# Gated cross-attention and quantised feed-forward on one core: the first two tiles laid out anew

## What is computed

```
q = Wq @ xn + bq            # [64, 512]
k = Wk @ cn + bk
v = Ws @ s + bs
attn = softmax(q^T k)       # [512, 512], over its last axis
mean = v @ attn^T ;  sq = (v*v) @ attn^T
x1 = x + tanh(g0) * (cn * sqrt(relu(sq - mean^2)) + mean)
x2 = x1 + tanh(g1) * layernorm(x1) @ w^T     # w = (weight_q - 8) * scale + zero, [512, 512]
```

## Time and profile before

| what | us |
|---|---|
| median of 3 runs (lowest to highest) | 186.06 (185.04 to 186.35) |
| the profiled execution's own time | 186.42 |
| its span, first to last instruction | 184.6 |
| busy: PE, DVE, ACT, POOL | 167.2, 141.0, 118.0, 120.4 |

### The profile page before, as it was taken

One profiled execution on the slowest core, in us unless ns is written; L12 is line 12 of the kernel. 1 busy time (PEld: TensorE's weight loads), 2 busy tenths in 40 slices (PEclk: granted clock), 3 DMA queues, 4 the chain that ended last, 5 costly groups with the idle time before them and its releaser, 6 DMA issues.

```text
span 184.6 us, 3489 instructions
## 1 busy us (share of the span) xinstructions
PE 167.2 (91%) x1128; PEld 147.1 (80%) x1128; DVE 141.0 (76%) x311; ACT 118.0 (64%) x261; POOL 120.4 (65%) x145
## 2 busy tenths in 40 slices
PE   1554999999999999999999999999999979789992
PEld 0432889999999999999999999998789867567881
DVE  2897696689859887986988798676159679988851
ACT  2253575978598678859867885995569995232110
POOL 1455586917955896799589679944328959966310
PEclk9999999999999999999999999999999999999999
DMA  6408566883796699679679966356100000111212
GB/s 169 166 21 202 186 159 138 237 201 86 184 319 153 155 287 245 162 216 286 139 170 249 283 145 153 78 134 151 44 0 0 4 0 0 57 62 60 111 57 114
DMA packets 14321, 25.75 MB, mean 139 GB/s; under 512 B 2336, under 2 KB 2464, under 8 KB 14304
## 3 DMA queue, kind: packets, MB, share of 16 engines
q1 hardware_dynamic: 14304, 25.54, 52.2%
HBM read 9.67 MB, written 2.10 MB: 64 GB/s over the span
## 4 chain that ended last, share of the span: by engine, by line
PE 76%; DVE 9%; ACT 4%; issue 4%; POOL 3%; DMA 2%; SPq 0%; ACTq 0%; POOLq 0%
PE pv_bank L322 28%; PE turn_bank L306 14%; PE score_bank L296 8%; PE score_bank L297 8%; PE side_bank L333 3%; PE score_bank L377 3%; PE score_bank L371 3%; PE score_bank L370 3%; DVE X L667 2%; DMA CTX<-in_context 2%; PE side_bank L342 2%; ACT probs L442 1%; PE side_bank L283 1%; DVE result L692 1%; DVE stats L673 1%
## 5 line engine op out<-in xcount | busy, mean ns | idle before, releaser
L831 POOL TENSOR_SCALAR probs<-probs,rden 128x512 f32<-128x512 f32 x64 | 50.9, 796 | 32.2 <-DVE rden L623 32.0
L322 PE MATMUL pv_bank<-probs_t,values 128*128 128x128 f32 x512 | 67.7, 276 | 0.0
L442 ACT ACTIVATE probs<-score_bank,neg_max 128x512 f32<-128x512 f32 x64 | 44.1, 690 | 31.4 <-DVE neg_max L616 30.8
L322 PEld LDWEIGHTS pv_bank<-probs_t,values 128*128 128x128 f32 x512 | 62.4, 192 | 2.1 <-issue 1.7
L616 DVE TENSOR_REDUCE neg_max<-score_bank 128x1 f32<-128x512 f32 x64 | 43.5, 682 | 15.0 <-PE score_bank L297 14.4
L306 PE MATMUL turn_bank<-ident,probs 128*128 128x128 f32 x256 | 38.8, 275 | 1.1 <-ACT probs_t L450 1.0
L450 ACT COPY probs_t<-turn_bank 128x512 f32<-128x512 f32 x64 | 37.1, 581 | 3.2 <-PE turn_bank L306 3.0
L306 PEld LDWEIGHTS turn_bank<-ident,probs 128*128 128x128 f32 x256 | 31.1, 142 | 5.7 <-POOL probs L831 1.1
L296 PE MATMUL score_bank<-c_both,q_both 128*128 128x512 f32 x64 | 29.3, 458 | 2.3 <-ACT q_with_x L494 2.3
L297 PE MATMUL score_bank<-c_with_bias,q_with_x 128*128 128x512 f32 x64 | 26.4, 412 | 0.0
L296 PEld LDWEIGHTS score_bank<-c_both,q_both 128*128 128x128 f32 x64 | 13.0, 202 | 4.6 <-issue 2.9
(11 more groups left out here) (99 smaller groups left out, 243.6 us busy)
## 6 DMA issues: line engine op xcount, KB each, us to landing
c_both<-c_hi SPq DMA_DIRECT2D x30, 128.0 KB, 2.6
X<-in_x SPq DMA_DIRECT2D x8, 256.0 KB, 3.0
CTX<-in_context SPq DMA_DIRECT2D x8, 256.0 KB, 4.1
ctx_now<-in_context SPq DMA_DIRECT2D x8, 256.0 KB, 2.9
sz<-in_scales_zeros SPq DMA_DIRECT2D x4, 512.0 KB, 6.7
out<-result SPq DMA_DIRECT2D x8, 256.0 KB, 2.0
q_with_x<-x_hi SPq DMA_DIRECT2D x15, 128.0 KB, 2.3
c_with_bias<-c_lo SPq DMA_DIRECT2D x15, 128.0 KB, 2.9
```

The lines of the kernel that those rows point to most:

```text
L322: last = pe.matmul(pv_bank[b][:, P * j:P * j + P], values[t % 2][:, i, b, :, :].rearrange("p a c -> p (a c)"), probs_t[g % PROBS_T][:, P * ...
L442: act.activation(probs[g % PROBS][:, :], score_bank[g % SBANKS][:, :], ACT.Exp, bias=neg_max[:, c:c + 1], accum_out=den[:, c:c + 1]).then_ ...
L831: pool.tensor_scalar(probs[g % PROBS][:, :], probs[g % PROBS][:, :], rden[:, c:c + 1], 1.0, ALU.mult, ALU.mult).then_inc(probs_done, 1)
```

## The change

The arithmetic of tiles 1 to 7 stays, apart from which engine casts. What differs:

- **Loads.** SP issues CTX0, X0, X1, CTX1, ctx_now0; params is issued by ACT as its first instruction. DVE takes the context's statistics first and x's second.
- **First projection.** `w_a` is kept in plain float32 (ACT copy), and `project_first` makes q of tile 0 as one fp32 product in two pieces, columns 0 to 127 into `turn_bank[1]` and 128 to 511 into `side_bank`. The split of `w_a` and tile 0's `x_hi`, `x_lo`, `c_hi` are gone from ahead of it; `w_a_hi` and `w_a_lo` are made on POOL after tile 0's `c_lo`, for `project(1)`.
- **First operands in place.** For tile 0 the engines write the stacked operands straight from their sources, q in pieces: batch 0 wholly, batch 1 the halves whose rows don't move. Four DMAs move the rest (before: seven). `first_lo` is DVE's part.
- **Order of PE.** Before the loop: `project_first` and scores 0 to 3. `value_product(0)` stands behind `turn(0)`, `project(1)` behind `turn(2)`, `project(2)` ahead of `turn(8)` (before: at chunk 7, ahead of `turn(7)`). From `project(3)` on the places are as before.
- **Order of the others.** DVE begins the softmax of chunk 0 among tile 1's statistics; normalising tile 1's context and values goes to chunk 0, `keep_q_lo(1)` to chunk 2, tile 2's preparation to chunks 4 to 7. The casts `x_hi` and `c_hi` of tiles 1 and 2 go from DVE to ACT (chunks 0, 1, 6, 7). POOL has `split_x_lo(1)` and `square_values(0)` in chunk 0, `split_c_lo(1)` in chunk 2, `split_x_lo(2)` and `split_c_lo(2)` in chunk 7.

Cut to its core (names of semaphores and their counts shift with it):

```diff
 SP
+            sp.dma_start(CTX[:, 0, :], context_tiles[0]).then_inc(first_loaded[0][1], DMA)
             sp.dma_start(X[:, 0, :], x_tiles[0]).then_inc(first_loaded[0][0], DMA)
-            sp.dma_start(params_sb[:, :], params).then_inc(params_loaded, DMA)
-            sp.dma_start(CTX[:, 0, :], context_tiles[0]).then_inc(first_loaded[0][1], DMA)
             load(1, *first_loaded[1])
             load_ctx_now(0)
+            sp.wait_ge(first_c_both, 3)
+            sp.dma_start(c_both[1][0:C, :].bitcast(F32), c_both[1][C:P, :].bitcast(F32)).then_inc(first_stacked, DMA)
+            sp.wait_ge(first_q_hi, 4)
+            sp.dma_start(q_both[1][0:C, :].bitcast(F32), q_hi[0][C:P, :].bitcast(F32)).then_inc(first_stacked, DMA)
+            sp.dma_start(q_with_x[1][0:C, :].bitcast(F32), q_hi[0][C:P, :].bitcast(F32)).then_inc(first_stacked, DMA)
             sp.wait_ge(c_lo_done, 1)
-            stack(0, 1, *x_and_context_copies)
-            sp.wait_ge(q_lo_done, 1)
-            stack(0, 1, *q_copies)
+            sp.dma_start(c_with_bias[1][0:C, :].bitcast(F32), c_lo[0][C:P, :].bitcast(F32)).then_inc(first_stacked, DMA)
             load_ctx_now(1)
             load(2, *first_loaded[2])
 PE
+            def project_first():
+                pe.wait_ge(xn_done, 1)
+                pe.wait_ge(w_a_ready, 1)
+                pe.matmul(turn_bank[1][:, FIRST], w_a[:, :], xn[:, FIRST], start=True, stop=True).then_inc(first_q_done, 1)
+                pe.matmul(side_bank[:, REST], w_a[:, :], xn[:, REST], start=True, stop=True).then_inc(first_q_done, 1)
...
             multiply_weights()
-            pe.wait_ge(w_split, 1)
-            project(0)
-            pe.wait_ge(bias_rows_ready, 2)
-            for g in range(AHEAD_S):
+            project_first()
+            for g in range(AHEAD_S + 1):
                 scores(g)
-            pe.wait_ge(q_lo_done, 1)
-            project(1)
-            scores(AHEAD_S)
-            value_product(0)
...
+                    if g == CHUNKS:
+                        pe.wait_ge(s_kept, 2)
+                        project(2)
                     turn(g)
+                    if g == 0:
+                        value_product(0)
+                    if g == 2:
+                        project(1)
 ACT, ahead of its loop
+            act.dma_start(params_sb[:, :], params).then_inc(params_loaded, DMA)
             act.wait_ge(w_turned_done, 1)
             act.copy(w_turned[:, :], turn_bank[0][:, 0:2 * P]).then_inc(w_turned_kept, 1)
+            act.wait_ge(ctxn_done, 1)
+            act.copy(c_both[0][0:C, :], CTX[0:C, 0, :]).then_inc(first_c_both, 1)
+            act.wait_ge(w_multiplied, 1)
+            act.copy(w_a[:, :], pv_bank[1][:, 0:P]).then_inc(w_a_ready, 1)
+            act.copy(c_both[0][C:P, :], CTX[0:C, 0, :]).then_inc(first_c_both, 1)
+            act.wait_ge(b_ready, 1)
+            act.wait_ge(first_q_done, 1)
+            act.activation(q_both[0][0:C, FIRST], turn_bank[1][0:C, FIRST], ACT.Identity,
+                           bias=b_a[0:C, 0:1]).then_inc(first_q_hi, 1)
+            act.wait_ge(first_q_hi, 1)
+            act.copy(q_with_x[0][0:C, FIRST], q_both[0][0:C, FIRST].bitcast(F32)).then_inc(first_q_copied, 1)
+            act.copy(c_both[1][C:P, :], CTX[C:P, 0, :]).then_inc(first_c_both, 1)
...
 ACT, in its loop, behind exponentials(g + 2) and keep_turned(g - 1)
+                    if g == 0:
+                        cast_x_hi(1)
+                    if g == 1:
+                        cast_c_hi(1)
+                    if g == 2:
+                        keep_q_hi(1)
...
 DVE, ahead of its loop
+            def first_lo(n, b, bank, columns, hi):
+                dve.wait_ge(first_q_hi, n)
+                dve.scalar_tensor_tensor(q_both[b][C:P, columns], bank[rows_of(b), columns], b_a[rows_of(b), 0:1],
+                                         hi[rows_of(b), columns].bitcast(F32), ALU.add,
+                                         ALU.subtract).then_inc(first_q_lo, 1)
...
+            dve.tensor_copy(q_with_x[0][C:P, :], xn[0:C, :]).then_inc(first_x_rows, 1)
+            first_lo(1, 0, turn_bank[1], FIRST, q_both[0])
             x_statistics(1)
+            first_lo(2, 0, side_bank, REST, q_both[0])
+            maximum(0)
             ctx_statistics(1)
+            maximum(1)
+            reciprocal(0)
             finish_statistics(1)
+            maximum(2)
+            reciprocal(1)
+            first_lo(3, 1, turn_bank[1], FIRST, q_hi[0])
+            first_lo(4, 1, side_bank, REST, q_hi[0])
             normalise_x(1)
-            keep_x_hi(1)
 DVE, in its loop, behind maximum(g + 3) and reciprocal(g + 2)
+                    if g == 0:
                         keep_values(0)
+                        normalise_ctx(1)
+                    if g == 2:
+                        keep_q_lo(1)
+                    if g == 4:
+                        keep_values(1)
+                        x_statistics(2)
+                    if g == 5:
+                        ctx_statistics(2)
+                        finish_statistics(2)
+                    if g == 6:
+                        normalise_x(2)
+                    if g == 7:
+                        normalise_ctx(2)
 POOL
+            pool.tensor_copy(w_a_hi[:, :], w_a[:, :]).then_inc(w_a_hi_ready, 1)
+            pool.wait_ge(w_a_hi_ready, 1)
+            pool.tensor_tensor(w_a_lo[:, :], w_a[:, :], w_a_hi[:, :].bitcast(F32), ALU.subtract).then_inc(w_split, 1)
+            normalise_probs(0)
             inverse_deviation(1)
+            normalise_probs(1)
...
+                    if g == 0:
+                        normalise_probs(2)
+                        split_x_lo(1)
                         square_values(0)
+                        pool.memset(averages[:, :], 1.0 / N).then_inc(consts_ready, 1)
+                        continue
+                    if g == 2:
+                        split_c_lo(1)
...
```

More of the change, by code:

```diff
@@ L60, in gated_attention_ffn @@
         w_turned = sb("w_turned", [P, 2 * P])
+        w_a = sb("w_a", [P, P])
         w_a_hi = sb("w_a_hi", [P, P], F32R)
@@ L190, in rows_of, with x_hi_of, c_hi_of @@
             return slice(C * b, C * b + C)
+        def x_hi_of(engine, t):
+            if t <= ACT_CASTS:
+                engine.wait_ge(x_hi_cast, t)
+            else:
+                engine.wait_ge(x_hi_done, t - ACT_CASTS)
+        def c_hi_of(engine, t):
+            if t <= ACT_CASTS:
+                engine.wait_ge(c_hi_cast, t)
+            else:
+                engine.wait_ge(c_hi_done, t - ACT_CASTS)
         def values_bank(t):
@@ L428, in keep_q_hi, with cast_x_hi, cast_c_hi @@
             def keep_q_hi(t):
[L430 to L433, removed]
-                act.activation(q_hi[t % 2][:, :], side_bank[:, :], ACT.Identity, bias=b_a[:, 0:1]).then_inc(q_hi_done, 1)
+                act.wait_ge(q_done, t)
+                if t == 2:
+                    act.wait_ge(first_stacked, 4 * DMA)
+                    act.wait_ge(first_q_lo, 4)
+                if t >= 3:
+                    act.wait_ge(stacked[0], STACK * (t - 2))
+                    act.wait_ge(stacked[1], STACK * (t - 2))
+                act.activation(q_hi[t % 2][:, :], side_bank[:, :], ACT.Identity, bias=b_a[:, 0:1]).then_inc(q_hi_done, 1)
+            def cast_x_hi(t):
+                act.wait_ge(xn_done, t + 1)
+                act.copy(x_hi[t % 2][:, :], xn[:, :]).then_inc(x_hi_cast, 1)
+            def cast_c_hi(t):
+                act.wait_ge(ctxn_done, t + 1)
+                act.copy(c_hi[t % 2][:, :], CTX[:, t, :]).then_inc(c_hi_cast, 1)
             def exponentials(g):
@@ L704, in _ @@
-            dve.tensor_copy(b_a[:, :], pv_bank[1][:, P:P + 2]).then_inc(b_ready, 1)
-            normalise_ctx(0)
-            dve.tensor_copy(q_with_x[0][C:P, :], x_hi[0][0:C, :].bitcast(F32)).then_inc(stacked[0], DMA)
-            keep_c_hi(0)
-            dve.wait_ge(c_hi_done, 1)
-            dve.tensor_tensor(c_with_bias[0][0:C, :], CTX[0:C, 0, :], c_hi[0][0:C, :].bitcast(F32),
-                              ALU.subtract).then_inc(stacked[0], DMA)
-            dve.wait_ge(q_hi_done, 1)
-            dve.scalar_tensor_tensor(q_both[0][C:P, :], side_bank[0:C, :], b_a[0:C, 0:1],
-                                     q_hi[0][0:C, :].bitcast(F32), ALU.add, ALU.subtract).then_inc(stacked[0], DMA)
@@ L720, in _ @@
             dve.wait_ge(gates_ready, 1)
-            for g in range(AHEAD_S):
-                maximum(g)
-                if g > 0:
-                    reciprocal(g - 1)
-            normalise_ctx(1)
-            keep_c_hi(1)
             for t in range(TILES):
@@ L887, in _ @@
             pool.tensor_copy(c_with_bias[1][C:P, :], b_a[C:P, 1:2].broadcast_to([C, N])).then_inc(bias_rows_ready, 1)
+            pool.wait_ge(xn_done, 1)
             pool.wait_ge(bias_rows_ready, 2)
-            split_c_lo(0)
-            inverse_deviation(1)
-            pool.memset(averages[:, :], 1.0 / N).then_inc(consts_ready, 1)
```

(18 more changed lines are left out.)

192 lines of the change are left out of this document (122 added, 70 removed).

## The result

| | us |
|---|---|
| kernel before, median of 4 (lowest to highest) | 186.2 (185.04 to 186.62) |
| changed kernel, median of 4 | 188.09 (187.75 to 188.63) |
| ratio, changed by before | 1.011, 95% interval 1.007 to 1.016 |
| span of the profiled execution, before and after | 184.6, 186.8 |

I had forecast 183.8. The change makes the kernel slower by 1.1%. The page of the changed kernel differs little as a whole: PE is busy for 1.5 us more, DVE 2.5 less, ACT 3.5 more (the earlier trace rows before); the two pairs of casts that moved from DVE to ACT are a part of it.

What follows compares the result with a forecast made beforehand. PE, busy 91%, was taken as the bound, the end set by when its closed row starts. A 2.85 us gain less 0.4 off 186.42 gave 184.0, or 183.6 from the median; stated 183.8, range 181.5 to 186.4.

Steps and rivals of the forecast that it cites:

- PE's closed row: PE's unbroken run of products up to the feed-forward; moving scores 8, first of tile 1, moves all behind by as much.
- The head: Tile 0 up to the first turn: scores 0 at 8.9 for 12.20 us, first turn at 13.35 for 21.62.
- the lead: PE's time won in tile 0: about 5.3 of the first turn's 8.3 us are real.
- Where the lead goes: Tile 1's operands: c_lo(1) ends at 21.0, SP's copies land at 27.3; scores 8 gains 2.85 us.
- the row of 1.92 us: Profile row of one long SP copy issue; forecast used it only for stack (1,1), landing by 32.7 us regardless.
- Behind scores 8: Tile 2's preparation: x_lo(2) at 33.65 where PE reaches project(2) at 33.25, 0.4 us lost; moved casts cost nothing to 0.6.
- The sum: Whole kernel: 2.85 - 0.4 = 2.45 us off the profiled execution's 186.42, giving 184.0; stated as 183.8.
- The shared ports: DVE and POOL lock each other out, 0.5 us a meeting in POOL's 5.1 us; three would leave 1 us gain.
- Rival 1: PE, not the stack, bounds scores 8, at 24.3 to 25.7 us; total 180.8 to 182.2; chance 0.14.
- Rival 2: Lead eaten: c_lo(1) at 22.2 to 23.8, scores 8 at 28.5 to 30.2; total 184.7 to 186.4; chance 0.25.
- Rival 3: PE's wait ahead of scores 8 lets its clock fall, costing 2.9 us; total 186.6 to 187; chance 0.08.

Runs made afterwards that it cites:

- e3: Changed kernel with SP issuing the x_hi and c_hi copies of stack (1, 0) ahead of c_lo; 185.49 us, ratio 0.997 to before.
- e5: Kernel before with the x_hi and c_hi copies of stack (1, 0) issued ahead of c_lo; 186.28 us, ratio 1.001 to before.
- e1: Changed kernel with tile 2's casts x_hi and c_hi moved back from ACT to DVE; 186.05 us, ratio 1.001 to before.
- e6: Changed kernel with tile 2's casts back on DVE and stack (1, 0)'s x_hi and c_hi copies issued early; 184.43 us, ratio 0.988 to before.
- e2: Changed kernel with tile 2's statistics and preparation ahead of maximum 8, casts still on ACT; 187.20 us, ratio 1.006 to before.
- e4: Changed kernel with tile 2's preparation ahead of maximum 8 and stack (1, 0)'s x_hi and c_hi copies issued early; 183.83 us, ratio 0.988 to before.

## Why the prediction was wrong

**What held.** That the start of PE's closed row sets the end held: behind `value_product(2)` nothing differs. But the row starts with `weigh` 8 at 42.85 and not with scores 8. The head held to 0.7 us: scores 0 at 8.9 by my sum and 9.49 measured, the first turn 13.35 and 14.08. The context's load landed at 4.00 for my 3.5, normalising to `xn` began at 7.01 for 6.35, and so the projection at 7.61 for 7.15; it then took 1.88 us for 1.7. PE came to scores 8 at 25.68, within my 24.3 to 25.7 (the sum there names five `weigh`/`value_product`; there are four, and with four it comes out). That batch 1's copies are in time, that the fp32 projection costs 0.4 us of PE and nothing at the end, and that the lead would end at SP's copies for tile 1, behind a `c_lo(1)` no earlier than before, held too; e3 and e5 show it from both sides.

**Where the lead goes: the size was off.** I put `c_lo(1)` at 21.0 and scores 8 at 27.35. Measured: 21.88 and 29.29. That is 1.94 us: 0.88 come with `c_lo(1)`, since POOL's row began at 16.68 for 15.85, and 1.23 are the one long issue of SP, less 0.2 of small differences. I had the row of 1.92 us before me, and let it weigh only on stack (1, 1), where there was slack. For stack (1, 0), which I had just made the bound, I used an undisturbed run of seven. The queue of before has seven such issues (1.17 to 2.00 us) in 138, so about one stack of seven in three meets one. That the profiled execution of the changed kernel met one in this very stack is bad luck in part: e1 had none there, and scores 8 came at 27.95, 0.6 us behind my sum.

**Behind scores 8: the step that failed.** "The casts moved to ACT cost ACT four times 0.6 us in chunks where it is busy three quarters; at nothing there, 0.6 if maximum and exponential are late." I priced the moved casts by their durations. They cost by what they wait for: ACT takes its instructions in order, so cast x_hi(2), placed ahead of exponential 9, held it for 2.03 us until DVE delivered `xn`, and then the mean and exponential 10. e6 against e3 puts 1.75 us on it, net of an `x_lo(2)` that comes 0.2 us later there. With `x_lo(2)` late by 0.79 (I had 0.4) and the rest of the waits, the stretch is 15.90 us, 2.99 above before, where I had added 0.4. The chain behind is the one that my text followed (maximum 8, statistics, power, `normalise_x(2)`, low part), but my text left out that it runs through ACT's queue.

**The sum.** +2.85 - 0.4 was the forecast; 0.90 - 2.99 = -2.09 was measured, and 0.1 from the tail, which is the 2.2 us between the spans. Of the 4.5 us between the two sums 1.95 lie up to scores 8 and 2.6 behind it.

**The shared ports**, priced at 0.5 us a meeting. The trace of the changed kernel agrees that such meetings occur: `normalise_x(2)` on DVE took 1.25 us (32.77) while POOL squared the values from 32.70 to 33.74, where it takes 0.54 alone; `normalise_ctx(1)` took 1.37 at 17.54 beside POOL's `split_x_lo(1)`. The Trainium skill's rule (SBUF — State Buffer, Who interferes with whom) has the later one wait; here that was DVE, not POOL as I had it, and with the casts behind it each of these delays went on to ACT. How much of the time hangs on it no run took apart.

**The rivals.** Rival 1 did not occur: PE was idle for 3.61 us. Rival 2 had scores 8 at 28.5 to 30.2, where it came, but by a `c_lo(1)` from 22.2 on; it ended at 21.88, and the long issue did the rest. Rival 2 also stopped at no gain. Rival 3, the clock, did not act in the changed kernel's profiled execution (1.00 from 25.6 to 45.2 us), but the clock fell in those of e1 and e2. There it cost the stretch 0.43 and 0.34 us, measured against e6 and e4, where the rival had 2.9. Its four executions have mean clocks of 1.00, 0.991, 1.00 and 0.99 and spans of 186.8, 186.0, 186.2 and 186.4: a lower mean goes with no longer span (and 0.991 can be the slow head alone, as e5 shows). So the clock is not why the kernel is slower. I gave 0.05 to slower by over 1%; what was missing was a case in which a new in-order wait adds to a stack that eats the lead.

## What to carry to other kernels

A step moved to an engine with spare time can cost that engine, and everything queued behind it, the wait for its input and not only its duration: look at what is next in the order there and whether the input can come earlier. When the head of a pipeline gets quicker, first move what feeds the second tile (here the copies whose sources exist early, and tile 2's statistics into the stretch where DVE is idle): the same head gave +1.9 us without this and -2.3 to -2.8 with it. A queue whose issue is sometimes three times as long should be summed with that row as well, once it is the bound.

## What the runs showed of the hardware

- An issue of one 128 KB copy on SP's queue took 1.2 to 2.0 us instead of 0.60, seven times among the 138 issues of the kernel before (the stores of the result aside) and four times among 134 in the changed one (1.37 to 1.83), 13 to 26 issues apart and not at the same copies. What causes it is open.
- PE idle for 2.53 and 2.86 us at 2.4 GHz was followed by a stretch at a granted clock of 0.50 (e1, e2), idle for 3.61 us in the changed kernel's profiled execution by none. After the falls in e1 and e2 the products were slow for some 3 us, not the 5.9 us that I took from the head. They were 1.6 us slower by it, but the stretches only 0.43 and 0.34 longer, as PE had waited there otherwise.
- In the kernel before the granted clock reads 1.00 where the spacing of products is that of 1.2 GHz (0.43 us for 512 columns up to 23.5 us): at the start of a span the record is no proof, the spacing is. With the same head the products had the spacing of 2.4 GHz by 11.10 us in e3 and from 17.1 us on in the changed kernel.
